# Two of each adapter unit's four quadrant loads issued by GpSimd from its own DMA queue

## The chip, the cores and the metric

The kernel runs on one core of a Trainium2 chip. Its engines are TensorE (PE in the profile), VectorE (DVE), ScalarE (ACT), GpSimd (POOL) and SyncE (SP). Each runs its own list of instructions in order and waits for the others on semaphores. The metric is the device time of one execution in microseconds.

## The reference

```python
x = x + _L0_cond_ref(x, L0_cond_W, L0_cond_b, condB_coeff, mask)
    # einsum('bsi,oi->bso', x, W) + b  +  einsum('bsi,bio->bso', x, 2*mask - 1) * coeff[:, None, None]
x = x + _L1_cond_ref(x, L1_cond_weight, itok_B_3_7)
    # w = weight[adapter_ids];  einsum('bsi,boi->bso', x, w)
```

x is 8 x 256 x 1024 float32, the mask 8 x 1024 x 1024 int32, W 1024 x 1024, and the adapter weights are eight matrices of 1024 x 1024, of which each batch b uses the one that its id names.

## The kernel before, in words

Per batch there are two products. The first, h = x (I + W^T + coeff * sign) + b, has as its weights one matrix per batch that is built on the chip: ScalarE turns a mask chunk into signs, VectorE multiplies by the coefficient and adds the transposed W (`add_sum`, L654), ScalarE rounds the sum to the 32-bit format of the fast multiply (`round_M`, L506), and VectorE takes the remainder (`rest_M`, L662), so that three products of rounded parts give the full precision. There are 8 chunks of 128 rows per batch, 64 in all; "mask n" is the n-th in the order of work. The second product, h (I + w^T), needs the adapter weights transposed.

The adapter weights come in 64 units, eight per batch: unit g is 128 output rows of the adapter of batch g // 8. `load_unit` (L224 to L227, SyncE) reads the adapter's id into a register and issues four DMAs of 128 KB, one for each quadrant of 32 partitions. The units go round a ring of four slots in the tile `natural`. GpSimd then adds 1 to the diagonal of a unit (`add_diagonal`, L320), which is the I in the product. VectorE transposes the unit in place in blocks of 32 (`turn_w`, L669), ScalarE rounds it (`round_w`, L521) and VectorE takes the remainder (`rest_w`, L673). The remainder ends the use of the slot: unit g's load waits for remainder g - 4. So three of VectorE's instructions matter below: the turn waits for the diagonal, the remainder frees the slot, and `rest_M` frees a mask tile.

Every engine's order is written out by hand. The first two batches are worked in an interleaved opening of 16 masks, in which the W chunks are turned too and two of the ring's slots (2 and 3) hold masks, so that units 2 and 3 wait for the remainders of masks 10 and 11 (`M_done` 11 and 12). From mask 16 on there is a loop: per mask one `add_sum`, `turn_w`, `rest_M` and `rest_w` on VectorE, and on TensorE the 24 matmuls of the first product (L387); a second product of 24 larger matmuls (L418) follows every second mask. TensorE starts the second product of batch 0 when its h is complete and four units are through (`w_done` 4), its right half at `w_done` 8; mask n's matmuls wait for `M_done` n + 1.

SyncE issues nearly all DMAs: masks, x, W, units and the stores of the result. GpSimd issues none; beside L320 it builds the identity and adds it to the eight chunks of W (L330).

Of the kernel before, what the change touches and what calls it, by code (L numbers as in the profile page):

```python
# [5 lines left out]
P = 128  # L6
SQ = 32
GRP = P // SQ
# [7 lines left out]
DMA = 16  # L16
RING = 4
# [12 lines left out]
def build(nc, x, coeff, ids, mask, W, bias, weight, out):  # L30
    B, S, D = x.shape
    K = D // P
    ST = S // P
    Q = D // GRP
    HALF = D // 2
    CHUNKS = B * K
# [12 lines left out]
    with ExitStack() as ctx:  # L49
        def sb(name, shape, dt):  # L50
            return ctx.enter_context(nc.sbuf_tensor(name, shape, dt))

        def sem(name):
            return ctx.enter_context(nc.semaphore(name))
# [5 lines left out]
        ids_row = sb("ids_row", [1, B], I32)  # L60

        natural = sb("natural", [P, RING, D], F32)
# [23 lines left out]
        ids_loaded = sem("ids_loaded")  # L86
        coeffs_loaded = sem("coeffs_loaded")
        bias_loaded = sem("bias_loaded")
        ident_steps = sem("ident_steps")
        natural_loaded = [sem(f"natural_loaded{i}") for i in range(RING)]  # L90
        mask_loaded = [sem(f"mask_loaded{i}") for i in range(OPEN_RING)]
        W_loaded = [sem(f"W_loaded{k}") for k in range(K)]
        x_loaded = [sem(f"x_loaded{half}") for half in range(2)]
# [7 lines left out]
        M_done = sem("M_done")  # L101
# [3 lines left out]
        w_done = sem("w_done")  # L105
        x_turned = sem("x_turned")
# [52 lines left out]
                    .rearrange("p u (c r) -> p u c r", r=SQ))  # L159

        def unit_landed(g):
            return DMA * GRP * (g // RING + 1)


        def x_arrives(b):
# [27 lines left out]
        def _(sp):  # L193
# [21 lines left out]
            def load_unit(g):  # L215
                if g == 0:
                    sp.wait_ge(ids_loaded, DMA)
                    sp.wait_ge(x_turned, 4)
                if g in (2, 3):

                    sp.wait_ge(M_done, 9 + g)
                if g >= RING:
                    sp.wait_ge(w_done, g - RING + 1)
                who = sp.value_load(ids_row[0:1, g // K:g // K + 1], min_val=0, max_val=weight.shape[0] - 1)  # L224
                m = g % K
                for a in range(GRP):
                    sp.dma_start(natural[a * SQ:(a + 1) * SQ, g % RING, :].rearrange("r (c f) -> r c f", f=Q),  # L227
                                 weight[bass.ds(who, 1), m * P:(m + 1) * P, a * Q:(a + 1) * Q]
                                 .rearrange("a (c r) f -> r (a c) f", r=SQ)).then_inc(natural_loaded[g % RING], DMA)
# [30 lines left out]
            load_mask(11)  # L260
            load_mask(12)
            load_unit(0)
            load_mask(13)
            load_mask(14)
            load_mask(15)
            load_unit(1)
            load_unit(2)
            load_unit(3)
            load_unit(4)
# [20 lines left out]
            for n in range(OPEN, CHUNKS + 2):  # L290
                b, i = n // K, n % K
# [18 lines left out]
        @block.gpsimd  # L310
        def _(pool):
            def add_diagonal(g):
                m = g % K
                at = slice(m // 2 * SQ, (m // 2 + 1) * SQ)
                row = natural[at, g % RING, m % 2 * P:m % 2 * P + SQ]
                one = ident[at, at]
                diag = bass.AP(row.tensor, row.offset, [row.ap[0], (Q + SQ, GRP), (1, SQ)])
                ones = bass.AP(one.tensor, one.offset, [one.ap[0], (0, GRP), (1, SQ)])
                pool.wait_ge(natural_loaded[g % RING], unit_landed(g))
                nc.gpsimd.tensor_tensor(diag, diag, ones, ALU.add).then_inc(w_diag_added, 1)  # L320

            nc.gpsimd.memset(ident[:, :], 0.0).then_inc(ident_steps, 1)
            pool.wait_ge(ident_steps, 1)
            nc.gpsimd.affine_select(out=ident[:, :], in_=ident[:, :], compare_op=ALU.not_equal, fill=1.0, base=0,
                                    pattern=[[-1, P]], channel_multiplier=1).then_inc(ident_steps, 1)
            pool.wait_ge(ident_steps, 2)
            for k in range(K):
                pool.wait_ge(W_loaded[k], DMA)
                diag = W_nat[:, k, k * P:(k + 1) * P]
                nc.gpsimd.tensor_tensor(diag, diag, ident[:, :], ALU.add).then_inc(W_diag_added, 1)  # L330
            pool.wait_ge(W_diag_added, K)
            for g in range(CHUNKS):
                if g:
                    pool.wait_ge(w_diag_added, g)
                add_diagonal(g)

        @block.tensor
        def _(pe):
# [35 lines left out]
            def products(b, k, parts_hi, parts_lo):  # L374
                hi, lo = x_part(x_hi, h_hi, b), x_part(x_lo, h_lo, b)
                (u0, M_h), (_, M_l) = parts_hi, parts_lo
                for v in range(M_h.shape[1]):
                    u = u0 + v
                    if b >= 2 and k == 0 and u % 2 == 0:

                        if b > 2:
                            pe.wait_ge(h_done, K * (b - 1) + u + 2)
                        elif u < 4:
                            pe.wait_ge(out_taken, 3 + u // 2)
                    for j, (left, right) in enumerate(((M_h[:, v, :], lo[:, k, :]), (M_h[:, v, :], hi[:, k, :]),
                                                       (M_l[:, v, :], hi[:, k, :]))):
                        done = nc.tensor.matmul(acc(b, u), left, right, start=(k == 0 and u % 2 == 0 and j == 0),  # L387
                                                stop=(k == K - 1 and u % 2 == 1 and j == 2))
                return done
# [257 lines left out]
        def _(dve):  # L647
# [9 lines left out]
            def rest_M(n):  # L657
                b, k = chunk_of(n)
                dve.wait_ge(M_hi_done, n + 1)
                whole = by_quadrant(mask_place(n)[0].bitcast(F32))  # L660
                for (u0, part), (_, rounded) in zip(M_lo_place(b, k), M_hi_place(b, k)):
                    done = nc.vector.tensor_tensor(  # L662
                        part.rearrange("p u (a j) -> p a u j", j=SQ), whole[:, :, u0:u0 + part.shape[1], :],
                        rounded.rearrange("p u (a j) -> p a u j", j=SQ).bitcast(F32), ALU.subtract)
                done.then_inc(M_done, 1)
# [141 lines left out]
```

## Time and profile before

| what | value |
|---|---|
| median of 3 runs | 404.85 us (403.4 to 412.76) |
| profiled execution | 403.49 us |
| its span, first to last instruction | 401.4 us |
| busy: TensorE, VectorE, ScalarE, GpSimd | 392.9, 352.3, 256.2, 53.7 us |
| moved by DMA | 88.56 MB, 221 GB/s on average, 374 GB/s in the second of 40 slices |
| unit loads | 256 DMAs of 128 KB, all on SyncE |

Busy time is that in which an engine executes an instruction; issuing a DMA does not count. Matmuls are pipelined, so their busy time overlaps and says less than the gaps do. An engine that is idle costs nothing unless the one that sets the end waits for it.

### The profile page before, as it was taken

Reading aid. Unit: us, or ns where it says so; the run is one execution under the profiler, and the core shown is the slowest. Engines: PE = TensorE matmul, PEld = TensorE weight load, DVE = VectorE, ACT = ScalarE, POOL = GpSimd, SP = SyncE. Lnnn points to the kernel's source line nnn. Section 1 sums busy time; section 2 is a strip of 40 time slices with the busy share of each in tenths; the row PEclk is TensorE's granted clock in tenths of the full one; section 3 lists DMA queues with packets and bytes.
Section 4 is the critical chain, followed back from the end, with each engine's and each line's share of the span. In section 5 each row is a group of like instructions: output and inputs, shape, how many; then the busy total and the mean of one; then the engine's idle time right before and its main releaser. Section 6 shows DMA issues by size and latency. Waiting matters only on the chain.

```text
span 401.4 us, 7261 instructions
## 1 busy us (share of the span) xinstructions
PE 392.9 (98%) x2578; PEld 359.8 (90%) x2578; DVE 352.3 (88%) x344; ACT 256.2 (64%) x321; POOL 53.7 (13%) x78
## 2 busy tenths in 40 slices
PE   7898999999999999999999999999999999999996
PEld 7898999888999999999999999999999999999885
DVE  0699899999999899989998999988998999988830
ACT  2799876766665766678566586656675685664521
POOL 1021110010021202110111111001000112111000
PEclk9999999999999999999999999999999999999999
DMA  8999877979999999999989996999579999745411
GB/s 224 374 314 315 300 153 195 236 186 249 260 251 251 232 234 232 255 215 225 206 258 223 233 225 219 257 251 250 146 214 243 221 220 210 223 132 149 140 52 52
DMA packets 64629, 88.56 MB, mean 221 GB/s; under 512 B 7250, under 2 KB 48210, under 8 KB 64594
## 3 DMA queue, kind: packets, MB, share of 16 engines
q1 hardware_dynamic: 63360, 88.10, 88.4%
q8 instruction: 20, 0.33, 0.4%
q10 hardware_dynamic: 1234, 0.01, 0.2%
q14 instruction: 15, 0.12, 0.1%
HBM read 79.70 MB, written 8.39 MB: 219 GB/s over the span
## 4 chain that ended last, share of the span: by engine, by line
PE 85%; DVE 9%; ACT 3%; DMA 2%; issue 1%; SPq 0%; DVEq 0%
PE second_ps L418 38%; PE first_ps L387 37%; PE first_ps L418 6%; PE turn_ps L370 3%; DVE masks L654 2%; DMA masks<-in_mask_Bx4096x_ik_dram 2%; ACT masks L491 1%; ACT WT L486 1%; DVE natural L669 1%; DVE M_lo L662 1%; DVE w_lo_left L673 1%; DVE h_lo L662 1%; DVE h_lo L685 1%; DVE w_lo_right L662 1%; PE turn_ps L350 1%
## 5 line engine op out<-in xcount | busy, mean ns | idle before, releaser
L387 PE MATMUL first_ps<-x_lo,M_hi 128*128 128x256 f32 x416 | 118.4, 285 | 0.0
L387 PE MATMUL first_ps<-x_hi,M_lo 128*128 128x256 f32 x416 | 117.7, 283 | 0.0
L387 PE MATMUL first_ps<-x_hi,M_hi 128*128 128x256 f32 x416 | 117.7, 283 | 0.0
L506 ACT CAST M_hi<-masks 128x1024 fp32r<-128x1024 f32 (+1 forms) x57 | 57.6, 1011 | 79.7 <-DVE masks L654 42.1
L654 DVE SCALAR_TENSOR_TENSOR masks<-masks,coeffs,WT 128x1024 f32<-128x1024 f32 x60 | 77.0, 1290 | 13.5 <-ACT WT L486 13.5
L320 POOL TENSOR_TENSOR natural<-natural,ident 32x128 f32<-32x128 f32 x64 | 46.7, 730 | 289.2 <-DMA natural<-in_L_cond_weight_dram 289.2
L387 PEld LDWEIGHTS first_ps<-x_lo,M_hi 128*128 128x128 f32 x416 | 79.7, 192 | 1.1 <-ACT out_sb L544 0.2
L387 PEld LDWEIGHTS first_ps<-x_hi,M_hi 128*128 128x128 f32 x416 | 79.7, 192 | 0.9
L387 PEld LDWEIGHTS first_ps<-x_hi,M_lo 128*128 128x128 f32 x416 | 79.7, 192 | 0.0
L669 DVE STREAM_TRANSPOSE natural<-natural 128x1024 f32<-128x1024 f32 x64 | 78.7, 1232 | 0.7 <-POOL natural L320 0.7
L662 DVE TENSOR_TENSOR M_lo<-masks,M_hi 128x1024 fp32r<-128x1024 f32 (+1 forms) x57 | 66.5, 1166 | 10.9 <-ACT M_hi L506 10.9
L491 ACT ACTIVATE masks<-masks 128x1024 f32<-128x1024 int32 x60 | 62.8, 1055 | 3.5 <-DMA masks<-in_mask_Bx4096x_ik_dram 3.5
L521 ACT CAST w_hi_left<-natural 128x1024 fp32r<-128x1024 f32 x32 | 33.6, 1050 | 18.1 <-DVE natural L669 17.6
L418 PE MATMUL second_ps<-w_hi_right,h_lo 128*128 128x512 f32 x112 | 44.1, 394 | 0.0
L418 PE MATMUL second_ps<-w_hi_right,h_hi 128*128 128x512 f32 x112 | 43.7, 391 | 0.0
L418 PE MATMUL second_ps<-w_hi_left,h_lo 128*128 128x512 f32 x112 | 43.7, 390 | 0.0
L418 PE MATMUL second_ps<-w_hi_left,h_hi 128*128 128x512 f32 x112 | 43.7, 390 | 0.0
L418 PE MATMUL second_ps<-w_lo_right,h_hi 128*128 128x512 f32 x112 | 43.7, 390 | 0.0
L418 PE MATMUL second_ps<-w_lo_left,h_hi 128*128 128x512 f32 x112 | 43.6, 389 | 0.0
L673 DVE TENSOR_TENSOR w_lo_right<-natural,w_hi_right 128x1024 fp32r<-128x1024 f32 x32 | 42.0, 1316 | 0.7 <-ACT w_hi_right L521 0.7
L673 DVE TENSOR_TENSOR w_lo_left<-natural,w_hi_left 128x1024 fp32r<-128x1024 f32 x32 | 41.3, 1292 | 0.3 <-ACT w_hi_left L521 0.2
L521 ACT CAST w_hi_right<-natural 128x1024 fp32r<-128x1024 f32 x32 | 33.6, 1054 | 8.9 <-DVE natural L669 6.5
(77 smaller groups left out, 542.9 us busy)
## 6 DMA issues: line engine op xcount, KB each, us to landing
natural<-in_L_cond_weight_dram SPq DMA_DIRECT2D x256, 128.0 KB, 5.6
masks<-in_mask_Bx4096x_ik_dram SPq DMA_DIRECT2D x60, 512.0 KB, 9.1
out_dram<-out_sb SPq DMA_DIRECT2D x32, 256.0 KB, 4.7
x_nat<-in_x_dram SPq DMA_DIRECT2D x14, 512.0 KB, 7.5
W_nat<-in_L_cond_W_dram SPq DMA_DIRECT2D x8, 512.0 KB, 8.1
natural<-in_mask_Bx4096x_ik_dram SPq DMA_DIRECT2D x4, 512.0 KB, 8.9
natural<-in_x_dram SPq DMA_DIRECT2D x2, 512.0 KB, 9.6
bias_col<-in_L_cond_b_dram ACTq DMA_DIRECT2D x4, 1.0 KB, 6.8
```

Source lines behind the costliest of these rows:

```text
L320: nc.gpsimd.tensor_tensor(diag, diag, ones, ALU.add).then_inc(w_diag_added, 1)
L350: done = nc.tensor.transpose(turned_W[:, t * P:(t + 1) * P], W_nat[:, k, t * P:(t + 1) * P], ident[:, :])
L370: done = nc.tensor.transpose(turned_x[:, k, s * P:(s + 1) * P], x_arrives(b)[:, s, at:at + P], ident[:, :])
L387: done = nc.tensor.matmul(acc(b, u), left, right, start=(k == 0 and u % 2 == 0 and j == 0), stop=(k == K - 1 and u % 2 == 1 and j == 2))
L418: done = nc.tensor.matmul(out_ps(b, t), left, right, start=(u == 0 and j == 0), stop=(u == K - 1 and j == 2))
L491: nc.scalar.activation(tile.bitcast(F32), tile, ACT.Copy, scale=2.0, bias=-1.0).then_inc(sign_done, 1)
L506: done = nc.scalar.copy(part.rearrange("p u (a j) -> p a u j", j=SQ), whole[:, :, u0:u0 + part.shape[1], :])
L521: nc.scalar.copy(w_part(w_hi, g), turned_unit(g)).then_inc(w_hi_done, 1)
L654: nc.vector.scalar_tensor_tensor(out=tile, in0=tile, scalar=coeffs[:, b:b + 1], in1=WT[:, k, :], op0=ALU.mult, op1=ALU.add).then_inc(sum_d ...
L662: done = nc.vector.tensor_tensor(part.rearrange("p u (a j) -> p a u j", j=SQ), whole[:, :, u0:u0 + part.shape[1], :], rounded.rearrange("p ...
L669: nc.vector.transpose(natural[:, g % RING, :], natural[:, g % RING, :]).then_inc(w_turned, 1)
L673: nc.vector.tensor_tensor(w_part(w_lo, g), turned_unit(g), w_part(w_hi, g).bitcast(F32), ALU.subtract).then_inc(w_done, 1)
```

## The change

SyncE issues quadrants 0 and 1 of each unit, GpSimd quadrants 2 and 3, from its own DMA queue and on a semaphore of their own for each ring slot. The diagonal waits for both semaphores. GpSimd loads the id itself, with the same waits as SyncE's load.

```diff
         def unit_landed(g):
-            return DMA * GRP * (g // RING + 1)
+            return DMA * GRP // 2 * (g // RING + 1)
 ...
-                for a in range(GRP):
+                for a in range(GRP // 2):
                     sp.dma_start(natural[a * SQ:(a + 1) * SQ, g % RING, :].rearrange("r (c f) -> r c f", f=Q),
 ...
                 pool.wait_ge(natural_loaded[g % RING], unit_landed(g))
+                pool.wait_ge(natural_rest_loaded[g % RING], unit_landed(g))
                 nc.gpsimd.tensor_tensor(diag, diag, ones, ALU.add).then_inc(w_diag_added, 1)
+
+            def load_unit_rest(g):
+                if g in (2, 3):
+
+                    pool.wait_ge(M_done, 9 + g)
+                if g >= RING:
+                    pool.wait_ge(w_done, g - RING + 1)
+                who = pool.value_load(ids_row[0:1, g // K:g // K + 1], min_val=0, max_val=weight.shape[0] - 1)
+                m = g % K
+                for a in range(GRP // 2, GRP):
+                    nc.gpsimd.dma_start(natural[a * SQ:(a + 1) * SQ, g % RING, :].rearrange("r (c f) -> r c f", f=Q),
+                                        weight[bass.ds(who, 1), m * P:(m + 1) * P, a * Q:(a + 1) * Q]
+                                        .rearrange("a (c r) f -> r (a c) f", r=SQ)
+                                        ).then_inc(natural_rest_loaded[g % RING], DMA)
 ...
             pool.wait_ge(W_diag_added, K)
+            pool.wait_ge(ids_loaded, DMA)
+
+            pool.wait_ge(x_turned, 4)
+            for g in range(RING):
+                load_unit_rest(g)
             for g in range(CHUNKS):
                 if g:
                     pool.wait_ge(w_diag_added, g)
                 add_diagonal(g)
+                if g >= 1 and g + 3 < CHUNKS:
+                    load_unit_rest(g + 3)
```

GpSimd's list before, from the last W diagonal on (L330), through the diagonals of units 0 to 4 (L320):

```order
L330 TENSOR_TENSOR W_nat<-W_nat,ident 128x128 [waits W_loaded7]
L320 TENSOR_TENSOR natural<-natural,ident 32x4x32 [waits natural_loaded0,W_diag_added]
L320 TENSOR_TENSOR natural<-natural,ident 32x4x32 [waits natural_loaded1,w_diag_added]
L320 TENSOR_TENSOR natural<-natural,ident 32x4x32 [waits natural_loaded2,w_diag_added]
L320 TENSOR_TENSOR natural<-natural,ident 32x4x32 [waits natural_loaded3,w_diag_added]
L320 TENSOR_TENSOR natural<-natural,ident 32x4x32 [waits natural_loaded0,w_diag_added]
```

The same place in the changed kernel, from the load of unit 3 on (L330 and L333 are its lines of the load, L322 the diagonal); the loads of units 0 to 2, six rows each, stand ahead of it:

```order
L330 TENSOR_LOAD ids_row [waits M_done]
L330 ISA x2
L333 ISA
L333 DMA natural<-in_L1_cond_weight_dram 32x4x256
L333 ISA
L333 DMA natural<-in_L1_cond_weight_dram 32x4x256
L322 TENSOR_TENSOR natural<-natural,ident 32x4x32 [waits natural_rest_loaded0,natural_loaded0]
L322 TENSOR_TENSOR natural<-natural,ident 32x4x32 [waits natural_rest_loaded1,natural_loaded1,w_diag_added]
L330 TENSOR_LOAD ids_row [waits w_done]
L330 ISA x2
L333 ISA
L333 DMA natural<-in_L1_cond_weight_dram 32x4x256
```

Diagonals 0 and 1 now stand behind the loads of units 0 to 3. The last four rows, with one more DMA behind them, are the load of unit 4; it waits for remainder 0 and stands ahead of diagonal 2, and the pattern goes on so with one load between each two diagonals.

VectorE's list around the first turns, the same in both kernels (L669 the turn, L673 the remainder; the first row here is turn 1):

```order
L669 STREAM_TRANSPOSE natural<-natural 128x1024 [waits w_diag_added]
L673 TENSOR_TENSOR w_lo_left<-natural,w_hi_left 128x8x128 [waits w_hi_done]
L669 STREAM_TRANSPOSE natural<-natural 128x1024 [waits w_diag_added]
L662 TENSOR_TENSOR h_lo<-masks,h_hi 128x4x8x32 [waits M_hi_done]
L673 TENSOR_TENSOR w_lo_left<-natural,w_hi_left 128x8x128 [waits w_hi_done] x2
L669 STREAM_TRANSPOSE natural<-natural 128x1024 [waits w_diag_added]
```

Nothing moved here: remainder 0 stands right ahead of turn 2, and remainders 1 and 2 right ahead of turn 3.

## Rows read from the trace of the kernel before

**Rows 1.** Busy time by stretch: start:end, length, PE, PEld, DVE, ACT, POOL, clock, DMA, GB/s
```profile
74.00:100.00 26.00, 25.85 (x128) 21.73 (x129) 25.64 (x29) 16.34 (x24) 3.37 (x7) 1.00 0.93 222
100.00:390.00 290.00, 290.00 (x1855) 264.50 (x1854) 268.73 (x256) 185.15 (x229) 39.61 (x51) 1.00 0.91 216
```

**Rows 2.** Chain of waits that ended last: start us, us, what
```profile
49.56 1.21 DVE M_lo L662
...
74.15 11.19 PE first_ps L418 x48
...
98.04 4.02 PE first_ps L387 x31
```

**Rows 3.** Time line of VectorE, 50 to 101 us: start us, us, line, operation, count [idle before]
```profile
51.90 1.23 DVE L669 STREAM_TRANSPOSE natural<-natural 128x1024 f32<-128x1024 f32 x1
...
59.19 1.17 DVE L673 TENSOR_TENSOR w_lo_left<-natural,w_hi_left 128x1024 fp32r<-128x1024 f32 x1
60.29 1.23 DVE L669 STREAM_TRANSPOSE natural<-natural 128x1024 f32<-128x1024 f32 x1
...
62.55 2.34 DVE L673 TENSOR_TENSOR w_lo_left<-natural,w_hi_left 128x1024 fp32r<-128x1024 f32 x2
64.82 1.23 DVE L669 STREAM_TRANSPOSE natural<-natural 128x1024 f32<-128x1024 f32 x1
...
69.79 1.18 DVE L673 TENSOR_TENSOR w_lo_left<-natural,w_hi_left 128x1024 fp32r<-128x1024 f32 x1
...
74.02 1.23 DVE L669 STREAM_TRANSPOSE natural<-natural 128x1024 f32<-128x1024 f32 x1
75.18 2.59 DVE L673 TENSOR_TENSOR w_lo_right<-natural,w_hi_right 128x1024 fp32r<-128x1024 f32 x2
...
80.84 2.35 DVE L669 STREAM_TRANSPOSE natural<-natural 128x1024 f32<-128x1024 f32 x2
83.18 2.36 DVE L673 TENSOR_TENSOR w_lo_right<-natural,w_hi_right 128x1024 fp32r<-128x1024 f32 x2
85.89 1.25 DVE L669 STREAM_TRANSPOSE natural<-natural 128x1024 f32<-128x1024 f32 x1 [0.34 <-POOL natural L320]
...
90.48 1.21 DVE L673 TENSOR_TENSOR w_lo_left<-natural,w_hi_left 128x1024 fp32r<-128x1024 f32 x1
...
92.74 1.24 DVE L669 STREAM_TRANSPOSE natural<-natural 128x1024 f32<-128x1024 f32 x1
...
99.73 1.18 DVE L662 TENSOR_TENSOR M_lo<-masks,M_hi 128x1024 fp32r<-128x1024 f32 x1
```

**Rows 4.** Time line of GpSimd: its last diagonal of W
```profile
41.97 0.46 POOL L330 TENSOR_TENSOR W_nat<-W_nat,ident 128x128 f32<-128x128 f32 x1 [2.52 <-DMA W_nat<-in_L_cond_W_dram]
```

**Rows 5.** Time line of SyncE's queue: a mask's issue and a unit's four
```profile
63.43 0.43 SPq L205 DMA_DIRECT2D masks<-in_mask_Bx4096x_ik_dram  x1
64.63 1.81 SPq L227 DMA_DIRECT2D natural<-in_L_cond_weight_dram  x4
```

**Rows 6.** Instructions on the ring tile: ns min/median/max, first and last start; landing times
```profile
L227 SPq DMA_DIRECT2D natural<-in_L_cond_weight_dram x256: 316/317/1630, 41.6 to 373.9; - x128
L320 POOL TENSOR_TENSOR natural<-natural,ident x64: 448/535/1549, 47.9 to 377.9; 32x128 f32<-32x128 f32 x64
...
DMA to landing us min/median/max: 2.5/5.6/12.8
```

**Rows 7.** Groups on GpSimd from 20 to 45 us: busy us, mean ns
```profile
L330 POOL TENSOR_TENSOR W_nat<-W_nat,ident 128x128 f32<-128x128 f32 x5 | 4.9, 977 | 20.6 <-DMA W_nat<-in_L_cond_W_dram 20.6
```

**Rows 8.** Time line of VectorE in the loop: a remainder and two turns, with rows between
```profile
105.92 1.23 DVE L673 TENSOR_TENSOR w_lo_right<-natural,w_hi_right 128x1024 fp32r<-128x1024 f32 x1
...
113.21 1.23 DVE L669 STREAM_TRANSPOSE natural<-natural 128x1024 f32<-128x1024 f32 x1
```

**Rows 9.** Time line of VectorE and TensorE at the end
```profile
382.79 2.41 DVE L673 TENSOR_TENSOR w_lo_right<-natural,w_hi_right 128x1024 fp32r<-128x1024 f32 x2
...
387.18 0.39 PE L418 MATMUL second_ps<-w_hi_right,h_lo 128*128 128x512 f32 x1
```

More of the change, by code:

```diff
@@ L90, in build @@
         natural_loaded = [sem(f"natural_loaded{i}") for i in range(RING)]
+        natural_rest_loaded = [sem(f"natural_rest_loaded{i}") for i in range(RING)]
         mask_loaded = [sem(f"mask_loaded{i}") for i in range(OPEN_RING)]
```

## The prediction

> **What bounds the kernel now.** I read the busy time by stretch first. From 100 to 390 us TensorE is busy for 290.00 of 290 us at the full granted clock, VectorE for 268.73 and the DMA engines for a share of 0.91; from 74 to 100 us TensorE still has 25.85 of 26 us and VectorE 25.64 of 26 [rows 1]. So after 74 us only something that makes TensorE wait can cost time, and nothing that speeds a load can give any. Then the chain of waits: at 74.15 us it passes from VectorE to TensorE and stays there [rows 2]. Before that, from 49.56 us on, it runs along VectorE without a gap, because the opening has VectorE do the first units' turns beside the sums and remainders of the masks. The order of VectorE's time line is what has to be read, since it holds both the instruction that frees a ring slot (the remainder, L673) and the one that waits for GpSimd's diagonal (the turn, L669) [rows 3]. Two facts there carry everything: turn 2 (60.29) starts the moment remainder 0 (59.19) is through, and the remainder of mask 17 (99.73 plus 1.18, so 100.91) is finished just as TensorE, which began the 2.9 us of mask 16 at 98.04 [rows 2], comes to mask 17 at about 100.95. The slack of the mask chain there is nil, so every microsecond that VectorE loses between 50 and 100 us arrives at TensorE.
>
> **The change, part by part.** I number units and ring turns from 0, and write L for what GpSimd spends on its half of a unit, a for one diagonal.
>
> *SyncE loses 128 of 256 issues.* One costs it a quarter of 1.81 us, 0.45 us [rows 5]. Before, VectorE waited for a diagonal 0.34 us at 85.89 us [rows 3] and about as long once later, and it waits for no mask in the dense stretch. I cost this edit at nothing: TensorE's and VectorE's full rows cover it. If that cover were gone, it would return 128 times 0.45 us to a queue, not to the span.
>
> *GpSimd gains 64 id loads and 128 issues.* On SyncE the id load with its register work takes 0.77 us (from the end of a mask issue at 63.86 to 64.63) [rows 5]; I take the same for GpSimd. No DMA by GpSimd is in the trace. Lower end for one: SyncE's 0.45 us. Upper end: the longest single issue seen, 1.63 us [rows 6]. In between I choose by the nearest thing GpSimd does in software over 128 pieces, its 128x128 diagonals of the opening, 0.98 us on average [rows 7]: 1.0 us. So L = 0.77 + 2 x 1.0 = 2.8 us, with ends 1.7 and 4.0. a is 0.55 us, the median of L320 [rows 6]. Of the Trainium skill, the page "DMA: Bandwidth & Descriptors" (table of latencies) gives about 1 us to the first byte on this path against 0.6 us on SyncE's; no run here shows it yet, and set in for one issue it would give the same sum as my choice.
>
> *What waits behind it.* GpSimd works in order. In its new order the loads of units 0 to 3 stand ahead of diagonal 0, and then the load of unit g+3 stands ahead of diagonal g+1, itself behind a wait for remainder g-1. Walk:
>
> - GpSimd is free at 42.43 us [rows 4]. Loads 0 and 1 end at 48.0. Load 2 waits for the remainder of mask 10 (49.6), load 3 follows: 49.7 + 2L = 55.3; diagonal 0 ends 55.8. Turn 0 was at 51.90: **+3.9 us**.
> - Turn 2: remainder 0 ends, 0.1 us for the semaphore, L, a. It had followed at once: **+3.5 us**.
> - Turn 3: the same behind remainder 1, with remainder 2 (1.15 us) as cover: **+2.4 us**.
> - Turns 1, 4 and 6 are covered by the sums, mask remainders and biased sums ahead of them.
> - Turn 5: +0.4. Turn 7: +1.3 (load 9 behind remainder 5). Turn 8: +1.9 (load 10 behind remainder 6). Turn 9, one sum after turn 8 and behind load 11: +1.0. Turn 10: +2.4 (load 12 behind remainder 8, with one mask remainder as cover) [rows 3].
>
> Sum 16.9 us on VectorE by mask 17, and TensorE gets all of it: 9.8 of it already at its first weight product (74.15), the rest at the second half of batch 0's weights and at masks 16 and 17. The walk with the ends: 7.6 us at 0.45 an issue, 9.6 at 0.6, 12.9 at 0.8, 23.6 at 1.3, 32.3 at 1.63. The slope is steep because seven stalls hold two issues each and the first holds four.
>
> *Landing.* Unit 4's half is issued some 10 us before its diagonal can run, later ones earlier still; landings took 5.6 us by the median, 12.8 at most [rows 6]. Cost nothing, hidden by the stalls; a landing at the maximum would add 1 or 2 us once.
>
> *The steady loop.* A remainder ends at 107.15, and the turn that the load behind it can hold up, two turns on, starts at 113.21 [rows 8]: 6.1 us for L + a = 3.3. Free, up to 2.4 us an issue. VectorE's four instructions of a round take some 4.95 us, while TensorE needs about 5.7 per mask (2.9 for the mask, and half of a weight product, a quarter of the 11.19 us of two [rows 2]), so VectorE also regains its lead. The end: VectorE's last remainder ends at 385.20, TensorE takes those weights at 387.18 [rows 9]; 2.0 us of slack, and the last loads lie well ahead of their turns. Cost nothing.
>
> *The port.* The same diagonal takes 0.45 to 1.55 us [rows 6], so GpSimd is sometimes held up while VectorE is full. If issues were stretched likewise, by 1.1 us each, one would cost 2.1 us and the sum would be over 45 us. I leave that out of the sum, because at each of the big stalls VectorE stands still while GpSimd issues. The skill's page "SBUF — State Buffer" (Who interferes with whom) says that descriptor writing is starved by VectorE only in its two-port modes of copy, cast and tensor_scalar, and that two-input instructions hold up only GpSimd's reads. VectorE runs none of the former here. By the rule the stretch never comes; by the row alone it may.
>
> **The rivals.**
>
> *A, the forecast:* VectorE waits for GpSimd at turns 0, 2, 3, 7, 8 and 10, with an issue of 0.5 to 1.5 us: 8 to 28 us. Chance 0.68.
>
> *B, not slower.* GpSimd hands a DMA on as cheaply as SyncE does (0.45 us or less), so that the diagonals follow almost at once: 7.6 us or less, 411 us or less. It decides at 0.49 us an issue, where the walk gives 8.1 us, 2% of the median. For it: SyncE's rows. Against it: GpSimd needs 0.45 us for a quarter of the partitions even in its shortest instruction [rows 6]. Chance 0.14, of which 0.02 for a real gain; for that a hidden wait would have to exist that the full TensorE row denies.
>
> *C, the dear issue:* 1.6 us or more, by the port or by a long first DMA. 32 to 45 us in the opening, and above 2.4 us the loop too loses some each round: 436 to 450. Chance 0.11.
>
> *D, the DMA engines become the bound.* Their share is 0.91 already [rows 1]. If descriptors written by software made the work of the rings a fifth dearer, 0.91 x 1.2 = 1.09, and 290 us would stretch by 9%, 27 us, on top of the opening: about 447. Against it: the bytes and the 1 KB pieces are the same, and the engines have moved 374 GB/s in an early slice of the page, against 216 in the loop [rows 1]. Chance 0.07.
>
> **The numbers.** The profiled execution took 403.49 us, with a span of 401.4; the median of the three is 404.85, so it stands 0.3% under it. 403.5 + 16.9 = 420.4; I say 420.5. Low end: at 0.45 an issue 411.1, less 2 us for a stall that the walk overrates: 409. High end: 1.63 an issue gives 435.8, plus some for idle gaps of 4 to 5 us on TensorE around 65 to 84 us, in which its clock could fall (before, it never did while it worked: 1.00 in every stretch [rows 1]); 438. Within 2% of the median is about what a measurement of this kernel tells from no change. Faster by over 2%: 0.02. Within: 0.12. Slower: 0.86.
>
> **What would show it.** VectorE's waits for GpSimd's L322 should grow from 0.7 to some 17 us, eight or so times, all before 105 us; TensorE's idle time likewise, in stretches at about 65 to 84 us and 96 to 118 us, and none after 125 us. The chain of waits should run over GpSimd's DMA instructions between 50 and 110 us. The length of a GpSimd DMA gives the size: the walk's figure for it should hold within 2 us. I am wrong if VectorE finds its diagonals ready (B), if its waits are spread over the whole span (C or D), or if masks or weights land late while GpSimd is idle (D).

## The result, and the profile after

The changed kernel takes 417.99 us (median of 5 runs, 416.43 to 418.54) against 405.97 for the kernel before on the same chip: ratio 1.031, 95% interval 1.026 to 1.035. It is slower, as forecast, within the range, and by somewhat less than the 420.5 us predicted. All ratios, here and below, are against the kernel before on the same chip, with 95% intervals; they leave disturbed runs out, which the medians do not, so the two can differ by some tenths of a per cent. The profiled execution took 416.43 us with a span of 414.5, 13.1 us more than the 401.4 before.

Where those 13.1 us lie shows in the busy time by stretch (columns as in [rows 1]; the last line is the kernel before in the last stretch):

```profile
60.00:74.00 14.00, 10.19 (x71) 9.77 (x69) 8.89 (x9) 4.33 (x7) 4.22 (x8) 0.88 0.44 120
74.00:100.00 26.00, 24.69 (x128) 21.51 (x128) 23.84 (x34) 16.88 (x28) 9.34 (x16) 0.93 0.70 186
100.00:125.00 25.00, 22.31 (x127) 19.91 (x127) 23.18 (x21) 13.29 (x15) 9.43 (x16) 0.93 0.87 209
125.00:390.00 265.00, 265.00 (x1719) 242.70 (x1718) 249.39 (x239) 172.13 (x215) 98.23 (x142) 1.00 0.85 220
...
125.00:390.00 265.00, 265.00 (x1690) 241.46 (x1689) 244.26 (x236) 169.34 (x213) 35.95 (x47) 1.00 0.90 212
```

From 60 to 125 us TensorE and VectorE have gaps and the clock is below 1.00; from 125 us on TensorE is as full as before, although GpSimd is now busy for 98 us there instead of 36 (this view counts the time that GpSimd's own DMA instructions take). The share of the DMA engines fell in the loop, from 0.90 to 0.85. So nothing is lost where four fifths of the new issues are.

VectorE's time line (compare [rows 3]), the instructions that waited for a diagonal, with one remainder and the remainder of mask 17:

```profile
54.36 1.25 DVE L692 STREAM_TRANSPOSE natural<-natural 128x1024 f32<-128x1024 f32 x1 [2.40 <-POOL natural L322]
...
61.66 1.18 DVE L696 TENSOR_TENSOR w_lo_left<-natural,w_hi_left 128x1024 fp32r<-128x1024 f32 x1
66.16 1.25 DVE L692 STREAM_TRANSPOSE natural<-natural 128x1024 f32<-128x1024 f32 x1 [3.32 <-POOL natural L322]
...
72.57 1.25 DVE L692 STREAM_TRANSPOSE natural<-natural 128x1024 f32<-128x1024 f32 x1 [1.79 <-POOL natural L322]
...
94.92 1.25 DVE L692 STREAM_TRANSPOSE natural<-natural 128x1024 f32<-128x1024 f32 x1 [1.80 <-POOL natural L322]
...
97.68 1.25 DVE L692 STREAM_TRANSPOSE natural<-natural 128x1024 f32<-128x1024 f32 x1 [0.35 <-POOL natural L322]
...
104.11 1.25 DVE L692 STREAM_TRANSPOSE natural<-natural 128x1024 f32<-128x1024 f32 x1 [1.81 <-POOL natural L322]
...
111.11 1.29 DVE L685 TENSOR_TENSOR M_lo<-masks,M_hi 128x1024 fp32r<-128x1024 f32 x1
```

Turns 0, 2, 3, 8, 9 and 10: 2.40 + 3.32 + 1.79 + 1.80 + 0.35 + 1.81 = 11.5 us. The remainder of mask 17 ends at 112.40 instead of 100.91, 11.5 us later: every one of these waits went through to mask 17. Behind it VectorE waited for a diagonal four more times, 2.9 us in all, and TensorE had no gap from it.

What GpSimd did meanwhile, on its time line:

```profile
50.86 1.17 POOL L333 DMA_DIRECT2D natural<-in_L_cond_weight_dram  x2 [5.06 <-DVE M_lo L685]
52.67 1.17 POOL L333 DMA_DIRECT2D natural<-in_L_cond_weight_dram  x2 [0.65 <-issue]
53.85 0.48 POOL L322 TENSOR_TENSOR natural<-natural,ident 32x128 f32<-32x128 f32 x1
...
64.45 1.17 POOL L333 DMA_DIRECT2D natural<-in_L_cond_weight_dram  x2 [7.36 <-issue]
65.68 0.44 POOL L322 TENSOR_TENSOR natural<-natural,ident 32x128 f32<-32x128 f32 x1
...
87.28 1.17 POOL L333 DMA_DIRECT2D natural<-in_L_cond_weight_dram  x2 [0.26 <-issue]
88.46 0.48 POOL L322 TENSOR_TENSOR natural<-natural,ident 32x128 f32<-32x128 f32 x1
```

The loads of units 2 and 3 run back to back after mask 10's remainder, and diagonal 0 comes only then, at 53.85; turn 0 follows at 54.36. Remainder 0 ends at 62.84, the load of unit 4 issues from 64.45 to 65.62, diagonal 2 ends at 66.12 and turn 2 starts at 66.16. The last pair is a load (unit 9) that was already free to go when GpSimd reached it: only 0.26 us lie ahead of its first issue.

The chain of waits that ended last runs over GpSimd in between, and splits what GpSimd needs before the first issue (start us, us, what):

```profile
62.87 0.29 POOLq L330
...
63.19 0.15 POOLq L330
...
63.39 0.40 issue
63.79 0.06 POOLq L333
...
63.91 0.51 issue
...
64.47 0.06 POOL natural L333
...
70.00 0.15 POOLq L330
...
70.21 0.03 issue
```

The id load and its register work take 0.29 and 0.15 us, and with the gaps around them and ahead of the first issue 1.6 us pass from remainder 0 to the issue. At turn 2 this holds a gap of 0.40 us (63.39) that is 0.03 us at turn 3 (70.21); what it is stays open. At turns 3, 8 and 10, where GpSimd also waited for a remainder, 1.2 to 1.3 us pass. The instructions of the load on GpSimd (ns min/median/max, first and last start):

```profile
L333 POOL DMA_DIRECT2D natural<-in_L_cond_weight_dram x128: 550/550/690, 42.8 to 387.8; - x128
```

One issue takes 0.55 us, almost without spread.

Most of the remaining 1.6 us is TensorE's clock. Its first wait, and the clock in stretches of 2 us around it and at mask 17 (columns as above, each from its own view):

```profile
68.56 0.39 PE L410 MATMUL first_ps<-x_lo,h_hi 128*128 128x256 f32 x1 [3.00 <-DVE h_lo L685]
```

```profile
66.00:68.00 2.00, 0.00 (x0) 0.00 (x0) 1.84 (x2) 0.57 (x1) 0.12 (x1) 1.00 0.85 249
68.00:70.00 2.00, 1.44 (x8) 1.44 (x9) 2.00 (x3) 1.52 (x3) 0.00 (x0) 0.72 0.41 141
70.00:72.00 2.00, 2.00 (x11) 2.00 (x11) 0.78 (x1) 0.00 (x0) 1.04 (x2) 0.50 0.21 43
...
114.00:116.00 2.00, 2.00 (x11) 2.00 (x11) 2.00 (x3) 1.12 (x2) 1.14 (x3) 0.50 1.03 283
```

TensorE stood idle for 3.0 us, went on at the full clock, and was granted 0.5 of it (1.2 GHz) shortly after. The same happened at mask 17, behind an idle gap of 2.15 us, and that one counts, because TensorE is then itself the bound. First the start of mask 17 in the kernel before, then the mask's 24 matmuls in the chain of the changed kernel:

```profile
100.97 0.38 PE L387 MATMUL first_ps<-x_lo,M_hi 128*128 128x256 f32 x1
```

```profile
112.46 4.63 PE first_ps L410 x24
```

Before, the mask began at 100.97 and the next product followed at 104.10 in the chain, 3.1 us later; now it takes 4.63 us: 1.5 us more. 11.5 + 1.5 = 13.0, against 13.1 measured. The clock's share belongs to this profiled run; with the opening alone, below, it is absent.

### The profile page after: what moved, and what is told of

Its sections match the earlier page's. It is cut to its first block, busy times and chain, and to the rows that moved or that the text cites. A ratio compares the mean times of both kernels' runs of the same rounds, so it can differ in the third digit from the quotient of the medians.

```text
span 414.5 us, 7456 instructions
## 1 busy us (share of the span) xinstructions
PE 399.3 (96%) x2578; PEld 365.5 (88%) x2578; DVE 354.0 (85%) x344; ACT 256.5 (62%) x321; POOL 134.2 (32%) x206
## 3 DMA queue, kind: packets, MB, share of 16 engines
q0 software_dynamic: 6144, 16.79, 16.4%
## 4 chain that ended last, share of the span: by engine, by line
PE 75%; DVE 13%; DMA 3%; ACT 3%; issue 3%; POOL 1%; POOLq 1%; SPq 1%; DVEq 0%
PE second_ps L441 37%; PE first_ps L410 35%; DVE natural L692 3%; PE turn_ps L393 3%; DVE masks L677 2%; DMA natural<-in_L_cond_weight_dram 2%; DMA masks<-in_mask_Bx4096x_ik_dram 2%; DVE w_lo_left L696 2%; DVE h_lo L708 2%; ACT masks L514 1%; DVE M_lo L685 1%; DVE h_lo L685 1%; ACT WT L509 1%; DVE w_lo_right L696 1%; DVE x_lo L701 1%
## 5 line engine op out<-in xcount | busy, mean ns | idle before, releaser
L333 POOL DMA_DIRECT2D natural<-in_L_cond_weight_dram x128 | 70.6, 552 | 202.2 <-issue 176.3
L685 DVE TENSOR_TENSOR M_lo<-masks,M_hi 128x1024 fp32r<-128x1024 f32 (+1 forms) x57 | 66.9, 1174 | 10.1 <-ACT M_hi L529 10.1
L322 POOL TENSOR_TENSOR natural<-natural,ident 32x128 f32<-32x128 f32 x64 | 57.6, 900 | 23.6 <-DVE w_lo_left L696 7.6
L696 DVE TENSOR_TENSOR w_lo_right<-natural,w_hi_right 128x1024 fp32r<-128x1024 f32 x32 | 44.2, 1383 | 0.7 <-ACT w_hi_right L544 0.7
L696 DVE TENSOR_TENSOR w_lo_left<-natural,w_hi_left 128x1024 fp32r<-128x1024 f32 x32 | 40.3, 1262 | 0.1
```

The lines of the kernel that those rows point to most:

```text
L333: nc.gpsimd.dma_start(natural[a * SQ:(a + 1) * SQ, g % RING, :].rearrange("r (c f) -> r c f", f=Q), weight[bass.ds(who, 1), m * P:(m + 1) ...
L685: done = nc.vector.tensor_tensor(part.rearrange("p u (a j) -> p a u j", j=SQ), whole[:, :, u0:u0 + part.shape[1], :], rounded.rearrange("p ...
L696: nc.vector.tensor_tensor(w_part(w_lo, g), turned_unit(g), w_part(w_hi, g).bitcast(F32), ALU.subtract).then_inc(w_done, 1)
```

## The experiments

Three theories. O, the order: VectorE's turns wait because GpSimd is busy with a load that stands ahead of the diagonal. R, the rings: the second queue delays masks or weights, or costs the DMA engines more. W, the wait and the id load alone do it, not the issues.

### The diagonals ahead of the loads in the opening

```diff
-            for g in range(RING):
-                load_unit_rest(g)
+            load_unit_rest(0)
+            load_unit_rest(1)
             for g in range(CHUNKS):
 ...
                 add_diagonal(g)
-                if g >= 1 and g + 3 < CHUNKS:
-                    load_unit_rest(g + 3)
+                if g == 0:
+                    load_unit_rest(2)
+                    load_unit_rest(3)
+                if 2 <= g <= 11:
+                    load_unit_rest(g + 2)
+                if 11 <= g and g + 3 < CHUNKS:
+                    load_unit_rest(g + 3)
```

Expected: 

> GpSimd still issues two quadrants of every unit; only its order in the opening is changed: diagonal 0 stands ahead of the loads of units 2 and 3, and the loads of units 4 to 13 stand behind diagonals 2 to 11 instead of one place ahead. Theory O (the order: VectorE's turns wait because a load stands ahead of the diagonal): VectorE's waits for GpSimd fall from 14.3 us to under 2 us, TensorE's clock stays at 1.00 throughout, the span falls from 414.5 to 401 to 404 us, ratio to the kernel before 1.00 (0.995 to 1.01). Rival R (the second queue itself: its landings, or what its descriptors cost the DMA engines): the loads go the same way, so most of the 13 us stays, 411 us or more.

Measured: 411.33 us (407.42 to 414.41), ratio 1.016 (1.009 to 1.023). About half of the loss is gone. O's forecast missed: it said 1.00, at most 1.01. The median lies at R's bound and the fastest run well below it, so the runs spread too widely for either forecast, and the kernel was run again:

Expected: 

> The kernel with the diagonals ahead of the loads in the opening once more, since its first runs spread over 407.4 to 414.4 us and its profile was one of the long ones. Theory O plus a smaller part for the queue (unit 0's halves land late, at 53.7 us instead of 47.9): 407 to 408.5 us, with one wait of 1.5 us at turn 0 and the rest small, and mask waits only in the long runs. Theory O alone: 404 to 406. Rival R: 411 or more in all runs.

Measured: 409.96 us (407.82 to 411.76), ratio 1.014 (1.008 to 1.020), the profiled execution 407.82 with a span of 405.8. The median is 1.5 us above the range expected, and below R's 411, which two of the six runs pass. VectorE's waits in the profiled run before 100 us:

```profile
52.10 1.25 DVE L697 STREAM_TRANSPOSE natural<-natural 128x1024 f32<-128x1024 f32 x1 [0.35 <-POOL natural L322]
56.43 1.28 DVE L682 SCALAR_TENSOR_TENSOR masks<-masks,coeffs,WT 128x1024 f32<-128x1024 f32 x1 [0.73 <-ACT masks L519]
...
84.11 1.25 DVE L697 STREAM_TRANSPOSE natural<-natural 128x1024 f32<-128x1024 f32 x1 [0.70 <-POOL natural L322]
88.21 1.25 DVE L697 STREAM_TRANSPOSE natural<-natural 128x1024 f32<-128x1024 f32 x1 [0.50 <-POOL natural L322]
```

The waits of 1.8 to 3.3 us are gone, also the 1.5 us expected at turn 0; small ones of 0.35 to 0.73 us remain, 3.0 us in all, and the clock is 1.00. Later a mask came 2.1 us late (at 132.53), and TensorE, at the end of the chain from there, waited 0.97 us at 152 us. The order is the larger part; this run, the fastest of the six, keeps 4.4 us of span, which O does not explain.

### Waits and id loads, but no issues

The changed order; SyncE issues four quadrants, and `load_unit_rest` ends after the id load:

```diff
                 who = pool.value_load(ids_row[0:1, g // K:g // K + 1], min_val=0, max_val=weight.shape[0] - 1)
-                m = g % K
-                for a in range(GRP // 2, GRP):
-                    nc.gpsimd.dma_start(...)
```

Expected: 

> SyncE issues all four quadrants as in the kernel before; GpSimd keeps the changed order with its waits and its id loads, but issues no DMA. Theory O with the price mostly in the issues: the id load and its register work (0.47 us in records, more with gaps) and the diagonal (0.45) remain between remainder and turn: turn 2 waits about 1.2 us, turns 0, 8 and 10 some tenths, about 2.5 us in all, 407 to 409 us. Rival W (the cost is the wait and the id load, not the DMAs): 9 us or more of the 13 stay, 414 us or more. Rival R: nothing stays, 404 to 406.

Measured: 406.59 us (406.27 to 408.54), ratio 1.008 (1.003 to 1.013), span 404.3. Turn 2:

```profile
61.78 1.25 DVE L685 STREAM_TRANSPOSE natural<-natural 128x1024 f32<-128x1024 f32 x1 [1.20 <-POOL natural L321]
```

1.20 us, as O had it; the time is just under O's 407 to 409. W is refuted as the whole: in the spans it makes 2.9 us of the 13.1.

### One quadrant and four

```diff
-                for a in range(GRP // 2):
+                for a in range(3):
 ...
-                for a in range(GRP // 2, GRP):
+                for a in range(3, GRP):
```

with the counts of the two semaphores adjusted, and likewise with all four quadrants on GpSimd.

Expected, one quadrant: 

> Order as in the changed kernel, but GpSimd issues one quadrant of each unit and SyncE three. Theory O: L falls by one issue of 0.58 us (0.55 and its register work): turn 0 gains 1.2 us (two loads ahead of it), turns 2, 3, 8 and 10 each 0.6, so 3.5 us less, 414 to 415 us against 418. Rival R: the software queue carries half as much, so half of the 13 us goes, 411 us. Rival W: no change, 417 to 419.

Measured: 410.71 us (410.5 to 412.22), ratio 1.019 (1.016 to 1.022), span 408.5. The direction is O's, but the size is nearly twice what I expected, and R's forecast of 411 us was the nearer number. The waits tell the two apart. Turns 2 and 3:

```profile
64.22 1.25 DVE L695 STREAM_TRANSPOSE natural<-natural 128x1024 f32<-128x1024 f32 x1 [2.33 <-POOL natural L325]
...
70.01 1.25 DVE L695 STREAM_TRANSPOSE natural<-natural 128x1024 f32<-128x1024 f32 x1 [1.17 <-POOL natural L325]
```

With one issue less turn 2 lost 1.0 us (the issue's 0.58 and the gap of 0.40), turns 3, 8 and 10 0.6 each, turn 0 1.25 (2.40 to 1.15) and turn 9 its 0.35, so the waits fell by 4.4 us, to 7.0. The rest of the 6.0 us of span is the clock. Ahead of mask 17 TensorE had waited 1.2 us here against 2.15 in the changed kernel, and it kept the full clock; from the chain:

```profile
108.13 3.13 PE first_ps L413 x24
```

3.13 us for the mask, as in the kernel before, against 4.63. I had left that out of the forecast, as I had the 1.0 at turn 2.

Expected, four quadrants: 

> Order as in the changed kernel, but GpSimd issues all four quadrants of each unit and SyncE none. Theory O: L grows by two issues, 1.2 us: turn 0 loses 2.3 us more, turns 2, 3, 8, 9 and 10 about 1.2 each, and turns 5 and 7 begin to wait, so 9 to 12 us more, 427 to 430 us, all of it before 130 us. Rival R: the queue carries twice as much, another 13 us, but spread over the loop, where TensorE would start to idle. Rival W: no change, 418.

Measured: 429.62 us (427.55 to 431.29), ratio 1.063 (1.057 to 1.069), span 428.4. Turns 0 and 2:

```profile
57.53 1.25 DVE L678 STREAM_TRANSPOSE natural<-natural 128x1024 f32<-128x1024 f32 x1 [5.22 <-POOL natural L308]
...
69.97 1.25 DVE L678 STREAM_TRANSPOSE natural<-natural 128x1024 f32<-128x1024 f32 x1 [4.17 <-POOL natural L308]
```

Turns 5 and 7 wait too now (1.01 and 1.74 us), 22.9 us in all before 125 us, and TensorE has no gap from 125 to 380. So with 0, 1, 2 and 4 issues per unit in the same order the span grows by 2.9, 7.1, 13.1 and 27.0 us. If the queue's cost were spread over all units, as R had it, there would be growth in the loop, where there is none.

### The loop alone, and the opening alone

```diff
+        def sp_quads(g):
+            return GRP // 2 if g >= 14 else GRP
 ...
             def load_unit_rest(g):
+                if sp_quads(g) == GRP:
+                    return
```

The second kernel has g < 14 in its place.

Expected, the loop: 

> SyncE issues all four quadrants of units 0 to 13; from unit 14 on GpSimd issues two and SyncE two, in the changed kernel's order. Theory O (the whole cost lies where a load stands ahead of a diagonal that VectorE is about to need, that is in the opening): VectorE waits under 1 us for diagonals beyond the kernel before, TensorE idles nowhere between 74 and 390 us, span 401 to 403 us, ratio 1.00 (within 0.5%). Rival R (the software queue delays masks or weights in the loop too): waits for late masks like the 3.2 us one at 136 us of the run with diagonal 0 first, 405 us span or more, ratio 1.01.

Measured: 403.84 us (403.26 to 410.07, 12 runs), ratio 1.0005 (0.997 to 1.004), span 401.4 to the tenth that of the kernel before. Its loop:

```profile
125.00:380.00 255.00, 255.00 (x1646) 233.17 (x1645) 240.97 (x232) 166.47 (x209) 95.33 (x134) 1.00 0.83 218
```

TensorE full, the share of the DMA engines 0.83, where the kernel before has 0.93 in the same stretch. VectorE waited 2.1 us for diagonals in the whole run, 1.4 more than before, and TensorE felt none of it. GpSimd's issues cost nothing there, and R fails for the loop.

Expected, the opening: 

> The reverse: GpSimd issues two quadrants of units 0 to 13 in the changed order, SyncE all four from unit 14 on. Theory O: all of the cost stays, 416 to 419 us, the same six waits of VectorE (about 11.5 us). Rival R: the part that the loop pays goes, 411 us or less.

Measured: 416.28 us (416.06 to 416.45), ratio 1.029 (1.021 to 1.036), span 414.5. The waits of turns 0, 2, 3, 8, 9 and 10 are 2.39, 3.31, 1.79, 1.82, 0.35 and 1.83 us, those of the changed kernel one by one. The equal span is in part chance, though: TensorE kept the full clock at mask 17 here, and waited 1.09 us later on, at the end of a chain that starts with a mask and a unit that landed late around 140 us:

```profile
112.71 0.39 PE L419 MATMUL first_ps<-x_lo,M_hi 128*128 128x256 f32 x1 [2.04 <-DVE M_lo L694]
...
160.71 0.38 PE L419 MATMUL first_ps<-x_lo,M_hi 128*128 128x256 f32 x1 [1.09 <-DVE M_lo L694]
```

The 11.5 us of waits belong to the 14 first units, two DMAs each; the other 50 units are free.

### The id read once per batch

```diff
-                who = pool.value_load(...)
+                if g % K == 0:
+                    held[0] = pool.value_load(...)
+                who = held[0]
```

Expected: 

> The changed kernel, but GpSimd reads the adapter's id into its register once for each batch, not once for each unit. Theory O with L made of an id load, two issues and gaps: where the id load ran after the wait (turns 2, 3, 8, 10) each stall falls by the load's 0.47 us and its gaps, 0.6 us; turn 0 falls by 0.6; in all 2.5 to 3.5 us less, 414.5 to 416 us. Rival (the id load is hidden behind the wait, only the two issues count): 418 us.

Measured: 414.08 us (410.92 to 415.62), ratio 1.022 (1.014 to 1.031), span 411.7. The waits are 1.23, 2.36, 1.57, 1.23 and 1.23 us, 7.6 instead of 11.5: 3.9 us less, where I expected 2.5 to 3.5. At turns 8 and 10 the id load was worth 0.6 us, as expected and more than its records of 0.44; at turn 2 0.96, since the gap of 0.40 went with it, and at turn 3 only 0.2, where a gap of 0.43 opened between the two issues. The span fell by only 2.8 us, because TensorE waited 2.33 us at 158 us behind a mask that came 2.5 us late.

### Diagonal 0 alone

Only `if g == 0: load_unit_rest(2); load_unit_rest(3)` behind diagonal 0; all else as changed.

Expected: 

> The changed kernel with one instruction moved: diagonal 0 stands ahead of the loads of units 2 and 3, all else as changed. Theory O, term by term: turn 0's wait falls from 2.4 us to 0.4 or less, the waits at turns 2, 3, 8 and 10 stay at 3.3, 1.8, 1.8 and 1.8; 2 to 2.5 us less than the changed kernel, 415 to 416 us. If the terms were not additive (a later wait takes the place of the first), 418.

Measured: 415.17 us (413.44 to 415.57), ratio 1.025 (1.016 to 1.034), span 411.5. Turn 0 waits no more, and the others are 3.34, 1.79, 1.81, 0.35 and 1.81 us, as they were. The waits add up as the walk has them. TensorE kept the full clock at mask 17 behind a gap of 2.07 us.

### The better order without issues

The kernel with the diagonals first, with waits and id loads on GpSimd and all DMAs on SyncE.

Expected: 

> The order with the diagonals first in the opening, with GpSimd's waits and id loads in their places, but no DMA by GpSimd: SyncE issues all four quadrants. It asks what the 3 to 6 us are that this order still costs with two issues. If the queue or the time of its two issues: 403.5 to 405 us, ratio 1.00 to 1.005. If the waits and id loads in this order: 407 us or more, ratio 1.01.

Measured: 404.05 us (403.28 to 410.98, 12 runs), ratio 1.000 (0.996 to 1.004). So in that order the waits and id loads are free within 0.4%, and its rest of 1.4% comes with GpSimd's issues, in the opening if the loop is free here as it was above. Whether through the 1.2 us of GpSimd's time or through later landings is not separated. In the trace of the better order 1.8 of the 3.0 us of waits stand behind something that landed late: a mask at 56.43, and the units of the turns at 70.14 and 84.11. The late mask of that trace around 132 us is not the issues' doing alone: in this kernel's profiled run, where GpSimd issues nothing, a mask came 2.2 us late at 130.25, and TensorE waited at the end of the chain from there:

```profile
150.19 0.39 PE L408 MATMUL first_ps<-x_lo,M_hi 128*128 128x256 f32 x1 [1.29 <-DVE M_lo L683]
```

No kernel tried beats the kernel before.

### One sum for all profiled runs

If the account above is right, each span grows by how much later mask 17 starts than at 100.97, plus what a lower clock adds in it and just behind it, plus TensorE's later waits (us):

| kernel | mask 17 later | clock | later waits | sum | span |
|---|---|---|---|---|---|
| changed | 11.5 | 1.5 | 0 | 13.0 | 13.1 |
| waits and id loads only | 2.2 | 0 | 0.5 | 2.7 | 2.9 |
| one quadrant | 7.2 | 0 | 0 | 7.2 | 7.1 |
| four quadrants | 23.3 | 2.7 | 0.6 | 26.6 | 27.0 |
| opening alone | 11.7 | 0 | 1.1 | 12.8 | 13.1 |
| id once per batch | 7.7 | 0 | 2.3 | 10.0 | 10.3 |
| diagonals first | 3.2 | 0 | 1.0 | 4.2 | 4.4 |
| diagonal 0 alone | 9.3 | 0 | 0.6 | 9.9 | 10.1 |
| diagonals first, no issue | 0.8 | 0 | 1.3 | 2.1 | 2.5 |

The first column follows VectorE's waits. The other two are not the same from kernel to kernel, and their causes were not tested.

## Why the prediction was right, and where its terms were off

- **That GpSimd's order in the opening decides**, and TensorE gets all that VectorE loses by mask 17: right. 11.5 us on VectorE, 11.5 us at mask 17. The waits came in six turns, not eight. Moving diagonal 0, or leaving the opening to SyncE, takes away just the terms named.
- **One issue, 1.0 us chosen between 0.45 and 1.63:** it is 0.55, 0.58 with its register work. The choice by the 128x128 diagonals, 0.98 us [rows 7], was mis-sized by 0.4. The test that I had set myself, that the walk's figure for the measured issue holds within 2 us, failed: for 0.58 us the walk gives some 9.3 us, and the waits were 11.5.
- **The id load, 0.77 us as on SyncE:** behind a wait for a remainder 1.2 to 1.3 us pass before the first issue, 1.6 at turn 2. There the two errors cancel by luck: 1.6 + 2 x 0.58 = 2.8 us, the 2.8 of the walk, and turn 2 came out at 3.32 against 3.5. At turns 3 and 10 L was 2.4, and the waits were 1.8 instead of 2.4 each; turn 8, with 1.80 against 1.9, was right.
- **The same L everywhere:** wrong, and this is why 16.9 us became 11.5. Where GpSimd comes to a load whose wait is already over, 0.26 to 0.65 us stand ahead of its issues, not 1.2 to 1.6. So turn 0, with two loads back to back, waited 2.40 instead of 3.9, turns 5 and 7 waited nothing instead of 0.4 and 1.3, and turn 9 waited 0.35 instead of 1.0.
- **The clock:** it stood only in the range. It is a term, 1.5 us at mask 17 in the profiled run, and absent in other kernels.
- **The number** is near in part by luck. The waits were 5.4 us too large in the sum, 1.5 us of clock were left out of it, and the median of the kernel before is now 2.5 us above the 403.5 that I added to. Against the growth of 13.1 us the 16.9 is 3.8 too many.
- **The loop, the landing and the end at nothing:** right. With GpSimd issuing in the loop alone the span is that of the kernel before. The loads that landed late around 130 to 140 us and cost TensorE 0.6 to 2.3 us in several of the kernels tried were in no term; in the changed kernel's profile TensorE waited for none.
- **The port:** the issue took 550 ns at the minimum and the median, 690 at most, and VectorE is busy 94% of the time in the loop. Beside VectorE's sums, which read two tiles in SBUF, two issues took their usual 1.17 us and a diagonal 1.32, where those that VectorE stood waiting for took 0.44 to 0.48:

```profile
96.33 1.32 POOL L322 TENSOR_TENSOR natural<-natural,ident 32x128 f32<-32x128 f32 x1
...
107.62 1.28 DVE L677 SCALAR_TENSOR_TENSOR masks<-masks,coeffs,WT 128x1024 f32<-128x1024 f32 x1
...
107.72 1.17 POOL L333 DMA_DIRECT2D natural<-in_L_cond_weight_dram  x2 [3.63 <-DVE w_lo_left L696]
```

The rule of the Trainium skill's page "SBUF — State Buffer" (Who interferes with whom) held: VectorE's instructions here do not hold up descriptor writing, and the diagonal beside a two-input one took longer. VectorE's two-port modes, which the rule is about, do not occur here.

- **The rivals:** B missed by little. The issue cost 0.58 us, near its turning point of 0.49; the walk gives 2.3% of the median for it, and the longer start of the load and the clock made it 3.1%. D was wrong in sign: the share of the DMA engines fell.

## What to carry to other kernels

A queue that an engine issues for is part of that engine's order: a DMA moved to an engine with compute of its own delays what stands behind it, wait included. Read, for each load moved, what is next on that engine and when its consumer needs it; here, in a steady loop with 6 us of room, 2.4 us and a diagonal were free, and in the dense opening they were paid for at every turn that followed the freeing remainder closely. If such a load must move, put it behind the work that someone waits for, or leave the opening to the engine that has nothing else to do.

## What was not expected of the hardware

The second queue, which the profile calls software_dynamic, moves the same bytes in fewer packets and with less time of the DMA engines (queue, kind: packets, MB, share of 16 engines). After:

```profile
q1 hardware_dynamic: 44928, 71.32, 63.2%
q0 software_dynamic: 6144, 16.79, 16.4%
```

Before:

```profile
q1 hardware_dynamic: 63360, 88.10, 88.4%
```

16.79 MB in 6144 packets are 2.7 KB each, where the removed 128 DMAs accounted for 18432 packets of SyncE's queue (63360 before), 0.9 KB each. Before, SyncE's queue held 88.10 MB at 88.4% of 401.4 us, 354.8 us; after, 262.0 us, so 92.9 us for the 16.78 MB that left it. The software queue took 68.0 us for them, 27% less. This takes the other packets to have cost what they did before; the three profiled kernels in which SyncE issues all range from 352 to 359 us, so the 27% is uncertain by some 3 points. With all four quadrants on GpSimd it is 33.57 MB in 12288 packets at 32.8% of 428.4 us, 70 us for each half. Here TensorE is the bound and it brings nothing; in a kernel bound by small pieces on the DMA engines it might, which no run here shows.

In the changed kernel TensorE's clock fell to 1.2 GHz three times, behind idle gaps of 3.0, 2.1 and 2.15 us, and in the kernel before in no stretch in which TensorE worked. At mask 17 the clock fell behind 2.15 us of idling, and stayed at 1.00 behind 2.04 and 2.07 us with the opening alone and with diagonal 0 alone; what makes the difference no run here tells. Short waits can thus cost more than their length: the 4.4 us of waits between one and two issues per unit were 6.0 us of span.
